# Three units of gated rows and two of active rows, group 14's rows on two queues and the attention weights behind them

## What is computed

```python
    # L0_ffn, 64 slots: expert products and the combination
    y = jnp.einsum('sio,bsi->bso', fc2_weight, y) + fc2_bias
    out = jnp.einsum('bsd,bst->btd', y, combine_w)
    # L1_attn
    q = (x @ Wq).reshape(B, N, 2, H, D).transpose(2, 0, 3, 1, 4)
    k = (x @ Wk).reshape(B, N, 2, H, D).transpose(2, 0, 3, 1, 4)
    v = (x @ Wv).reshape(B, N, H, D).transpose(0, 2, 1, 3)
    # L1_ffn, 8 segments of 64 small experts, 4 of them chosen per token and segment
    z = jnp.einsum('nd,sdr->nsr', xf, P)
    scores = jnp.einsum('nsr,smr->nsm', z, C)
    topv, topi = jax.lax.top_k(scores, K)
    w = jax.nn.softmax(topv, axis=-1)
    h = jax.nn.gelu(jnp.einsum('nsr,nskrh->nskh', z, W1g) + b1g)
    yl = jnp.einsum('nskh,nskhr->nskr', h, W2g) + b2g
    comb = jnp.einsum('nskr,nsk->nsr', yl, w)
    out = jax.nn.gelu(comb @ G1 + g1b) @ G2 + g2b
```

## Time and profile before

| | us |
|---|---|
| median of 3 runs | 833.26 |
| lowest, highest | 831.75, 839.11 |
| the profiled execution | 830.03 |
| its span from first to last instruction | 828.2 |

### The profile page before, as it was taken

The page is one execution under the profiler, slowest core; times in us unless marked ns, Lnnn a source line. Parts: engine busy times, 40 slices in busy tenths (PEclk is TensorE's granted clock), DMA queues, the critical chain, the costliest instruction groups (busy, mean ns, idle before and its releaser), DMA issues.

```text
span 828.2 us, 15472 instructions
## 1 busy us (share of the span) xinstructions
PE 682.1 (82%) x6032; PEld 363.6 (44%) x6032; DVE 501.0 (60%) x1195; ACT 346.9 (42%) x587; POOL 143.0 (17%) x153
## 2 busy tenths in 40 slices
PE   5999999899787677798889889987787969778971
PEld 3666666544333333456657566552122213222220
DVE  5578777711111110148686777967787877869966
ACT  0433434242211210133433334446776867758840
POOL 0040403401000000050050204525312021200002
PEclk9899999999988999879997999999797988999995
DMA  7810101449999999810010291379896988889941
GB/s 286 350 45 2 45 2 38 193 178 423 426 408 403 426 426 373 163 52 2 1 40 1 33 119 24 81 265 355 273 361 208 374 296 285 293 345 386 419 171 45
DMA packets 42322, 178.40 MB, mean 215 GB/s; under 512 B 6495, under 2 KB 20771, under 8 KB 37795
## 3 DMA queue, kind: packets, MB, share of 16 engines
q1 hardware_dynamic: 41878, 177.45, 59.9%
q10 hardware_dynamic: 384, 0.15, 0.1%
HBM read 170.09 MB, written 7.29 MB: 214 GB/s over the span
## 4 chain that ended last, share of the span: by engine, by line
PE 38%; DVE 23%; DMA 20%; issue 7%; ACT 4%; POOL 3%; SPq 3%; ACTq 1%; DVEq 0%; POOLq 0%
DMA early<-gate_dram 8%; DMA stream<-in_fc_dram 7%; DVE work L2197 5%; PE P L370 4%; DMA early<-in_patches_dram 3%; PE P L442 3%; PE P L2104 3%; PE P L842 3%; PE P L875 3%; PE P L413 2%; PE P L833 2%; PE P L2079 2%; PE P L850 2%; ACT work L2164 2%; PE P L426 2%
## 5 line engine op out<-in xcount | busy, mean ns | idle before, releaser
L2164 ACT ACTIVATE work<-P 128x768 f32<-128x768 f32 (+1 forms) x192 | 147.7, 833 | 37.1 <-PE P L2079 36.7
L2197 DVE TENSOR_TENSOR work<-work,early 128x1536 f32<-128x1536 f32 (+1 forms) x77 | 139.7, 1825 | 32.4 <-ACT work L2164 17.9
L2104 PE MATMUL P<-work,stream 128*32 128x384 f32 (+1 forms) x768 | 91.5, 551 | 27.8 <-DVE work L2197 27.0
L2079 PE MATMUL P<-early,stream 99*128 99x384 bf16 (+1 forms) x384 | 90.7, 359 | 16.8 <-ACT work L2164 16.6
L524 ACT ACTIVATE work<-work 101x444 f32<-101x444 f32 x48 | 28.1, 586 | 115.4 <-DVE work L519 115.4
L2079 PEld LDWEIGHTS P<-early,stream 99*128 99x128 bf16 x384 | 31.8, 102 | 95.9 <-ACT work L2164 68.6
L928 DVE COPY work<-P 128x768 f32<-128x768 f32 x16 | 15.3, 958 | 89.1 <-PE P L859 89.1
L911 ACT ACTIVATE work<-P 128x768 f32<-128x768 f32 x16 | 13.0, 811 | 128.0 <-PE P L850 128.0
L620 POOL TENSOR_SCALAR work<-work 101x4 f32<-101x4 f32 x12 | 2.7, 228 | 359.8 <-DVE work L610 359.8
L442 PE MATMUL P<-work 101*37 101x34 f32 x1152 | 45.7, 206 | 4.5 <-DVE work L566 2.5
L442 PEld LDWEIGHTS P<-work 101*37 101x37 f32 x1152 | 40.8, 120 | 12.9 <-issue 6.5
(11 more groups left out here) (248 smaller groups left out, 1159.4 us busy)
## 6 DMA issues: line engine op xcount, KB each, us to landing
early<-gate_dram SPq DMA_DIRECT2D x51, 768.0 KB, 5.9
stream<-in_fc_dram SPq DMA_DIRECT2D x14, 2304.0 KB
stream<-in_fc_dram SPq DMA_DIRECT2D x15, 1536.0 KB, 9.5
early<-gate_dram SPq DMA_DIRECT2D x26, 832.0 KB, 8.2
stream<-in_fc_dram SPq DMA_DIRECT2D x15, 768.0 KB, 11.0
work<-gate_dram SPq DMA_DIRECT2D x13, 768.0 KB, 6.6
work<-gate_dram SPq DMA_DIRECT2D x6, 832.0 KB, 8.2
early<-in_patches_dram SPq DMA_DIRECT2D x4, 888.0 KB, 4.9
```

Of the source, the lines that this page charges most:

```text
L2079: mm = pe.matmul(P[:, hidden_bank(p) + j, 0:WIDE[c]], w1s[:, seg, (hh * (CH // 2) + i) * 128:(hh * (CH // 2) + i + 1) * 128], zs[c][:, seg ...
L2104: mm = pe.matmul(P[32 * j:32 * j + 32, 6 + sq, 0:WIDE[c]], w2[:, hh * (CH // 2) + i, 4 * sq + j, :], gated[:, 4 * (g % 2) + j, 0:WIDE[c]], ...
L2164: act.activation(act_out[:, 2 * (p % 6):2 * (p % 6) + 2, 0:cols], P[:, hidden_bank(p):hidden_bank(p) + 2, 0:cols], ACT.Gelu_apprx_tanh).th ...
L2197: dve.tensor_tensor(gated[:, at:at + 4, 0:cols], act_out[:, 4 * (g % 3):4 * (g % 3) + 4, 0:cols], spread_gates(g), ALU.mult).then_inc(s_ug, 1)
```

## The change

Handover: SP and ScalarE now place half of each of groups 14 and 15, eight DMAs each. SP does this before it loads the attention's weights. TensorE's wait for the weights moves from ahead of the `combine` products to behind them and two `keep_busy` products, ahead of `pe_turn`.

Units: `gated` gets 12 rows (three units), `act_out` 8 (two units); the fourth place of the gate ring moves from behind `gated` to behind `act_out`. The product's wait for `s_u2` is gone; the product of unit 2, the first in the third slot, waits for the last `h_out`, which VectorE itself makes. ScalarE's first half of unit g waits for product g - 2 from unit 2 on; its second half waits for no product.

```diff
-        gated = tenant(work, 128, 0, [8, 416])
-        act_out = tenant(work, 128, shared, [12, 416])
+        gated = tenant(work, 128, 0, [12, 416])
+        act_out = tenant(work, 128, shared, [8, 416])
...
-        spread_at = ((early, 0), (early, 1664), (early, 8640), (work, 3328), (early, 3328))
+        spread_at = ((early, 0), (early, 1664), (early, 8640), (work, shared + 8 * 416), (early, 3328))
...
             gather(GROUPS - 2, SLOTS - 4 * GS, SLOTS - 2 * GS)
+            for g in (GROUPS - 2, GROUPS - 1):
+                place(sp, g, (0, 1))
             sp.wait_ge(s_hid, GROUPS)
             for dst, name in ((w_q1, "w_q1"), (w_k1, "w_k1"), (w_v1, "w_v1"), (w_o1, "w_o1")):
                 sp.dma_start(dst, io[name]).then_inc(s_late, 16)
-            place(sp, GROUPS - 1, (0, 1))
...
-            place(act, GROUPS - 2, range(GS))
-            place(act, GROUPS - 1, (2, 3))
+            for g in (GROUPS - 2, GROUPS - 1):
+                place(act, g, (2, 3))
...
-            pe.wait_ge(s_late, 64)
             pe.wait_ge(s_y2, 16 * 20)
             for j in range(QP):
                 combine(0, j, (2, 3, 6, 7)[j])
             keep_busy(pe, 0, 2)
+            pe.wait_ge(s_late, 64)
             pe_turn(pe, L1, 0, h_in, L0["h_out"], QP, QUADS)
...
-                                   gated[:, 4 * (g % 2) + j, 0:WIDE[c]],
+                                   gated[:, 4 * (g % 3) + j, 0:WIDE[c]],
...
-                if g >= 3:
-
-                    act.wait_ge(s_ug, g - 2)
+                if g >= 2 and p % 2 == 0:
+
+                    act.wait_ge(s_ug, g - 1)
                 cols = WIDE[g // NG]
-                act.activation(act_out[:, 2 * (p % 6):2 * (p % 6) + 2, 0:cols], P[:, hidden_bank(p):hidden_bank(p) + 2, 0:cols],
+                act.activation(act_out[:, 2 * (p % 4):2 * (p % 4) + 2, 0:cols], P[:, hidden_bank(p):hidden_bank(p) + 2, 0:cols],
...
-                if g >= 2:
-
-                    dve.wait_ge(s_u2, g - 1)
-                at = 4 * (g % 2)
-                dve.tensor_tensor(gated[:, at:at + 4, 0:cols], act_out[:, 4 * (g % 3):4 * (g % 3) + 4, 0:cols], spread_gates(g),
+                if g == 2:
+
+                    dve.wait_ge(LO["h_out"], QP * QUADS)
+                at, to = 4 * (g % 2), 4 * (g % 3)
+                dve.tensor_tensor(gated[:, to:to + 4, 0:cols], act_out[:, at:at + 4, 0:cols], spread_gates(g),
                                   ALU.mult).then_inc(s_ug, 1)
```

## The result

The changed kernel takes 821.96 us (median of 4 runs, 818.74 to 826.24) against 832.5 us (4 runs); the ratio is 0.9876, with a 95% interval from 0.9828 to 0.9924. The same kernel was timed three more times in other sets, with ratios of 0.9889, 0.9872 and 0.9915. It is 10.5 us faster here and about 8 us faster over all sets, where 2.2 us were forecast; the forecast range ended at 827. A ratio leaves out executions more than 1.5% above the fastest of their kernel in the set, while the fits to single runs further down use all of them and rank the handover, the units and the whole alike without those (-5.3, -0.3 and -7.6 us). The profiled execution took 826.24 us, with a span of 824.4 us against 828.2 before, so it shows less of the gain than the times do: it copied group 14 at 340.63 us, where the profiled execution before copied it at 335.26, with nothing changed ahead of that point.

A forecast was written before the change was run, and what follows sets the result against it. No engine bounds the whole; at the handover the rows' landing sets the end. Rows 2.2 us earlier and units at 0 take the median of 833.26 us to 831.0, range 827.0 to 835.0.

The forecast's parts named there:

- Where the end is set: At the handover, the rows' landing at 348.59 us sets the end; the chain then runs unbroken to turning and projections.
- The landing time: Handover: rows land 4.1 us after the last issue, floor 3.7, ceiling 5.91; combining at 346.4, 2.2 us earlier.
- Which half of the handover pays: Handover: issuing on two queues gives 0.4 to 1.4 us; the rest comes from weights behind the rows.
- The rule on queues: Handover: DMA engines take queues with work in turn, so rows would not stand behind weights; the trace was said to disagree.
- a sign of being right: Handover: packets of ScalarE's queue would move from 341 us on or before.
- the rival built on the rule: Handover: landing time does not depend on what is ahead; 0.4 us by issue alone, 832.9 us; chance 0.15.
- The clock rival: Handover: shorter TensorE idleness keeps its clock up through the projections, 3.1 us more gained, 827.9 us; chance 0.08.
- The weights: Handover: loads issued later land at 351.6 us, hidden by 7.06 us of combining and normalising, 2 us to spare.
- the third unit of gated rows: Units: a third unit removes the wait for second products; priced at 0, between 0 and -3.0 us.
- the wait for second products: Units: VectorE's 3.0 us of waits go but gain 0; a rival counted them, 828.0 us, chance 0.08.
- Lockstep: Units: ScalarE and VectorE in lockstep, up to 7.6 us slower, 838.6 us; chance 0.11.
- the ring: Units: two units of active rows make ScalarE wait for product g-2; priced at 0, up to +7.6 us uncovered.

The follow-up runs named there:

- e2_units: Only the units part of the change, handover as in the kernel before; median 836.83 us against 837.53, six runs.
- e4_queues: Kernel before with rows of groups 14 and 15 split over SP and ScalarE, weights still ahead of them; ratio 0.9896, 831.21 us.
- e5_behind: Kernel before with SP's four weight loads behind its four row transfers and TensorE's wait moved, ScalarE still issuing twelve; ratio 1.003.
- after: Profile of the changed kernel, with the whole change against the kernel before; profiled execution 826.24 us, median 821.96.
- e16_whole: The whole change repeated in the fourth set, against the kernel before; ratio 0.9915, 826.73 us against 836.35.
- before: Profile of the kernel before, nothing changed; span 828.2 us, median 832.5 us of four runs.
- e9_before: The kernel before, unchanged, counted as a run of its own against the kernel before; ratio 1.0039.
- e10_handover: Only the handover part of the change, units as in the kernel before, third set; ratio 0.9979, 829.97 us against 833.35.
- e12_whole: The whole change repeated in the third set, against the kernel before; ratio 0.9872, 823.29 us.
- e15_ring: Kernel before plus the handover part and two units of active rows, gated rows left at two units; ratio 0.997, 829.38 us.

## Why the prediction was wrong

**Where the end is set** was right for the profile before, and for the one after: rows landing, then combining, normalising and turning without a break. That the handover pays was right as well; that only it does is not settled (the units alone +0.3 +- 1.4 us).

**The landing time was the mis-sized term.** I took 4.1 us from the last issue to the rows, with 3.7 as the floor, from loads of 64 and 256 KB that were issued while others moved. After the change the last of the eight issues starts at about 347.7 and combining at 349.97: some 2.3 us. A 12 KB row between two tiles of the chip, with little else moving (32 GB/s), needs about half of what those loads took. The nearest rows of the trace bounded the cost of a bigger thing under load, and I made their lower end a floor. These 1.8 us are the whole distance between the forecast and the profile up to there: combining +4.7 us after group 15's copy, against 346.4 - 339.87 = +6.5; the last issue started 2.5 us after that copy, against 2.4 forecast. The clock adds 1.25 us up to the turning (below). That makes 5.5 us against the profile of before where 2.2 were forecast; it does not explain all of the 7.8.

The reading behind the term was a little off as well: the 5.91 us of the earlier trace rows run from the start of the twelfth issue (342.68), not from the eleventh's, and even at that issue the landing is not a constant: with the same old order of queues and an earlier end of the gather (`e2_units`) combining came 2.6 us after the start of the last issue, although the weights stood ahead there too.

**Which half of the handover pays** I probably had the wrong way round. The forecast gave 0.4 to 1.4 us to the second queue and the rest to the weights' new place. Measured, the two queues with the weights still ahead (`e4_queues`) are worth 3.9 +- 1.8 us, and the weights moved behind, with ScalarE at twelve issues (`e5_behind`), 0.0 +- 1.7. The difference is 1.6 standard errors in the fit, while the ratios' intervals lie apart (0.9852 to 0.9939, 0.9983 to 1.0076). In the profiles `e4_queues` has its rows 3.2 us earlier after the copy than before, but only 0.7 earlier than `e2_units`, so by how much issue alone does this lies between these; and only both steps together reach +4.7. What the weights' place adds there is not in the rows' packets: the last of them ends 4.05 us after the copy in `e4_queues` and in `after` alike, and TensorE starts 1.75 us behind it in the one and 0.7 in the other.

**The rule on queues** stood beside a row that contradicted it, and the new rows go both ways. In `after`, ScalarE's queue, issued to from 341.02 on, has its first packet at 342.6, 1.55 us later and 2.0 us before the gather's last one ends; its last issue, with nothing of the gather ahead, took 1.27 us to its first packet, so here the gather held it up by 0.3 us at most. (Counted from the copy of group 14, that first packet came at 1.9 us, against 7.3 before, which was a sign of being right.) In `e5_behind` the first packet comes 1.27 us after the issue, 2.1 us before the gather's end. In `e16_whole`, issued to from 339.88, it comes at 344.7, 4.8 us later, as it came 6.9 us later before the change. The Trainium skill (DMA: Bandwidth & Descriptors, Queues, rings and completion order) has each DMA engine take the queues with work in turn. `after` and `e5_behind` agree with that; `before` and `e16_whole` do not, and what decides between them is open. Where the rival built on the rule went wrong in time is another matter: it gave 832.9, 0.4 us for the issues, and the measured time is 11 us below; but the second queue, all that it left standing, measured 3.9 +- 1.8 us.

**The clock rival** (0.08) was half right. Combining to turning did get faster by 1.25 us: after 1.2 us of idleness the granted clock is 0.98 there, after 5.4 us it was 0.52. The projections did not (11.49 us, at a clock of 0.72). I had named TensorE's idleness beside the normalisation as the reason that could hinder them; the runs don't show it to be that (8.24 us in `e16_whole` with 2.13 us of idleness there, 9.9 in `e5_behind` with 0.65). What I had not considered is that low stretches later on differ as well, in the attention and behind the units; that the handover sets them is likely and not shown.

**The gather** is what the prediction missed. The prediction reads the landing as issue plus a constant. In four of the ten profiles with the new order the gather ended 5 us after group 15's copy and the rows came 4.3 to 4.6 us after that, whatever their issues did. The trace of before showed the case on its edge, the gather ending 1.0 us after the copy.

**The weights** stayed hidden, as forecast: in `after` the turning was ended by VectorE (2.34 us of idleness, none for `stream`). **The units**: the third unit of gated rows is worth nothing that 18 runs can tell (+0.3 +- 1.4 us), the forecast being 0; the wait for second products went away, and VectorE's wait for ScalarE stayed. **Lockstep** (0.11) did not come: 170 to 174 us from unit 0 to 63 in all eighteen profiles, where it would have cost 7.6, though with ScalarE waiting 23.9 us for VectorE all the same. In time, the ring is at +2.4 +- 1.7 us alone (its twelve runs are 0.3 us slower on the mean than the twelve of `e9_before`) and +0.9 +- 2.0 on top of the handover.

**The range** was too narrow apart from all this. It was put together from terms of one execution, while single runs scatter by 5.3 us, and the mean granted clock of a run is mostly between 0.90 and 0.93, the longer runs having the lower clock. The range had no term for low stretches that fall elsewhere. Part of the miss is luck of the draw: the four runs of the result are 10.5 us faster than before, all sets together 7.8. What is left open: of the 7.8 us, the profiles account for 1.7 to 5.5 at the handover (by which profile of the old order the new ones are held against), and the rest (fewer low stretches in the attention, the shorter end behind the units, or chance) isn't settled.

## What to carry to other kernels

A transfer's time from issue to landing, read where queues are full, is neither a floor nor a constant: before costing a move, find the last packet of what was issued ahead of it, and see in what order the packets go. Splitting a dozen small issues over two queues was probably worth more here than moving 864 KB of weights out of their way, and only both together brought combining to 4.7 us after the last copy. Compare several executions of the kernel before to see on which side of such an edge it stands, and time a kernel against itself (here 1.0039 [0.9999, 1.0078]) before reading 0.4% into anything.

## What the runs showed of the hardware

- The gather's last 96 packets, 12 KB to one partition each, took 1.33 us on the mean before (1.15 to 1.31 in the other profiles), while the 9 KB packets of the expert weights took 0.35 us (median) on the same queue ahead: those 96 take 9.3 to 10.9 us, some 110 to 125 GB/s.
- A 12 KB row from tile to tile is there about 2.3 us after the start of its issue with little else moving (`after`), and 7.1 to 7.4 us after it with the gather's last packets ahead and weights behind (`e10_handover`, `e12_whole`, `e15_ring`, `e16_whole`).
- Where the last row packet ends at 344.0 (`e12_whole`), combining starts 3.3 us later; where little else moved until then (`after`), 0.7 us later. The delay is in the completion and not at TensorE: the last increment of the rows' semaphore comes at 347.21 in `e12_whole`, 3.2 us behind the packet, and at 349.88 in `after`, 0.6 us behind it. What holds it up is open; the weights' packets begin at 343.1 in the one, ahead of the rows' last, and at 349.3 in the other.
- The clock's low stretches lie elsewhere from profile to profile. Those with the rows on two queues and the old units are at the lower level from the last product with gates to the end; the changed kernel's fall to it 12 to 13 us behind that product. Here are `e10_handover` (last product's end at 791.6) and `e12_whole` (796.4):

```profile
792.00:812.00 20.00, 14.74 (x76) 6.56 (x68) 10.73 (x40) 1.11 (x2) 3.18 (x6) 0.50 0.10 23
```

```profile
800.00:805.00 5.00, 4.25 (x50) 2.88 (x52) 3.43 (x12) 0.25 (x1) 0.88 (x2) 1.00 0.00 0
```

The granted clock is 0.50 over 20 us in the first and 1.00 in the second. The end behind that product takes 30.0 us in the one and 26.6 in the other; these 3.4 us are more than the forecast gave to the whole change.
